# Latent attention: context products on unsplit F32 rows in column halves, with row sums added on DVE and POOL

## The reference

```python
B, S, L, H = 16, 100, 1444, 16           # batches, queries, keys, heads
D_CQ, D_C, R = 192, 64, 64
q_big = apply_rope(einsum('bshk,hkq->bshq', (x @ Wq.T), w_kc_q))
kv_r  = apply_rope(kv_c)                                   # (B, L, 64), shared by all heads
q_r = einsum('bshq,hqr->bhsr', q_big, W_qr)
k_r = einsum('bld,hdr->bhlr', kv_r, W_kr)
attn  = softmax(einsum('bhsr,bhlr->bhsl', q_r, k_r))
ctx_c = einsum('bhsl,bld->bhsd', attn, kv_r)               # per head 100 x 64
out   = (einsum('bhsd,hkd->bhsk', ctx_c, w_kc_kv)) @ Wo.T
```

## Time and profile before

| | us |
|---|---|
| median of 3 runs | 2277.09 (2274.82 to 2286.96) |
| the profiled execution | 2283.25, its span 2281.4 |
| latent queries | about 76 to 306 of the span |
| latent attention | about 308 to 1370, its first turn of maxima at 354.4 |
| PE busy over the span | 1857.9 (81%) |
| DVE, ACT, POOL busy | 1492.1, 1220.5, 1117.1 |
| mean granted TensorE clock | 0.905 of full speed |

### The profile page before, as it was taken

One profiled execution on the slowest core, in us unless ns is written; L12 is line 12 of the kernel. 1 busy time (PEld: TensorE's weight loads), 2 busy tenths in 40 slices (PEclk: granted clock), 3 DMA queues, 4 the chain that ended last, 5 costly groups with the idle time before them and its releaser, 6 DMA issues. The chain is left out here.

```text
span 2281.4 us, 38538 instructions
## 1 busy us (share of the span) xinstructions
PE 1857.9 (81%) x10550; PEld 1632.6 (72%) x10550; DVE 1492.1 (65%) x2799; ACT 1220.5 (53%) x2996; POOL 1117.1 (49%) x961
## 2 busy tenths in 40 slices
PE   4999958999999999999999973499993689837870
PEld 3677736888888888888888963499993466626870
DVE  4677777777777777767776433377774466656763
ACT  2111115777777767767777851366661266515650
POOL 0455528888788888878888852300004100014005
PEclk9999967999999999999999985699996599958985
DMA  5522251111111111111110002455542100026654
GB/s 159 197 58 57 55 176 55 63 63 63 45 54 63 64 31 63 63 64 63 63 54 11 16 8 78 140 197 196 204 165 58 34 1 0 0 77 196 198 164 113
DMA packets 115748, 195.76 MB, mean 86 GB/s; under 512 B 48213, under 2 KB 94265, under 8 KB 110161
## 3 DMA queue, kind: packets, MB, share of 16 engines
q1 hardware_dynamic: 107409, 180.88, 24.6%
q0 software_dynamic: 8192, 13.15, 2.0%
HBM read 147.01 MB, written 46.63 MB: 85 GB/s over the span
## 5 line engine op out<-in xcount | busy, mean ns | idle before, releaser
L501 POOL TENSOR_TENSOR EL<-E,EH 128x400 fp32r<-128x400 f32 x688 | 833.4, 1239 | 158.5 <-ACT EH L733 154.0
L599 DVE TENSOR_REDUCE PM<-bank 128x1 f32<-128x482 f32 (+1 forms) x624 | 397.2, 650 | 185.9 <-PE bank L578 182.9
L742 ACT ACTIVATE E<-bank 128x400 f32<-128x400 f32 x768 | 386.4, 503 | 212.8 <-PE bank L793 153.2
L733 ACT ACTIVATE EH<-E 128x400 fp32r<-128x400 f32 x768 | 407.0, 532 | 0.0
L175 PE MATMUL bank<-EH,KVH 128*128 128x400 f32 x768 | 283.1, 369 | 19.8 <-POOL EL L501 18.5
L578 PE MATMUL bank<-KH,QS 128*128 128x482 f32 (+1 forms) x624 | 250.9, 414 | 53.9 <-DVE KVL L549 27.6
L1248 POOL DMA_INDIRECT m_back<-rows_out,m_slots x64 | 64.8, 1013 | 450.8 <-DMA rows_out<-m_ys 421.2
L792 PE MATMUL bank<-QS,KH 128*128 128x400 f32 x768 | 272.1, 354 | 14.9 <-issue 9.1
L793 PE MATMUL bank<-QB,KB 66*128 66x400 f32 x768 | 269.1, 350 | 0.0
L175 PE MATMUL bank<-EH,KVL 128*128 128x400 f32 x768 | 265.7, 346 | 0.0
L175 PE MATMUL bank<-EL,KVH 128*128 128x400 f32 x768 | 265.5, 346 | 0.0
(11 more groups left out here) (244 smaller groups left out, 3983.3 us busy)
## 6 DMA issues: line engine op xcount, KB each, us to landing
m_stage_u<-in_m_up SPq DMA_DIRECT2D x20, 1392.0 KB
raw<-in_ctx_T SPq DMA_DIRECT2D x16, 1444.0 KB, 6.1
m_xg<-rows_in SPq DMA_DIRECT2D x55, 256.0 KB, 4.1
rows_out<-m_ys SPq DMA_DIRECT2D x55, 256.0 KB, 3.7
m_stage_d<-in_m_down SPq DMA_DIRECT2D x20, 696.0 KB
queries<-q_out SPq DMA_DIRECT2D x64, 200.0 KB, 2.4
QS<-queries SPq DMA_DIRECT2D x16, 800.0 KB, 6.1
rows_in<-zeros SPq DMA_DIRECT2D x5, 1792.0 KB
```

The lines of the kernel that those rows point to most:

```text
L501: ops.tensor_tensor(EL[:, n % PB, :], E[:, n % EB, :], as_f32(EH[:, n % PB, :]), ALU.subtract).then_inc(sem, 1)
L599: nc.vector.tensor_reduce(PM[:, f:f + 1], psum[F0 + f % f_banks(b)][:, 0:KW[f % KC]], AX.X, ALU.max).then_inc(red_done, 1)
L733: nc.scalar.activation(EH[:, n % PB, :], E[:, n % EB, :], ACT.Copy).then_inc(hi_done, 1)
L742: nc.scalar.activation(E[:, n % EB, :], psum[S0 + n % SB][:, 0:CH], ACT.Exp).then_inc(exp_done, 1)
```

## The change

- **Values** are plain F32: KV (rotated, unsplit) against the exponentials R, unsplit. A batch has two parts p of eight heads, NS = 24 steps of (p, key tile). Each step has two score tiles, one of the four even heads of the part and one of the odd ones, 400 columns each, read as strided heads from QS and QB. The value product of the even heads goes to partitions 0 to 63 of bank CTX, that of the odd heads to 64 to 127. Each has a 64-column stationary operand. High copies (L733), EL (L501) and the columns of ones go.
- **Row sums**: DVE adds the even heads' tiles one by one in a PSUM bank (ACC), POOL the odd heads' tiles in SBUF (EA). The last addition writes ES, and TensorE multiplies a matrix of ones (64 wide) with it, two F32 matmuls a part. ACT copies them to SU.
- **Padding keys** are switched off by a row of -1e30 in KB instead of the ones column.
- **Order**: TensorE works in groups of two steps: a pair of maximum pieces, four scores, a pair of maximum pieces, the values of the two steps before. Maximum pieces are all 482 wide (overlapping), and DVE reduces two in one instruction.
- **Rotation** of the keys moves from DVE to POOL, but for two parts; the division is one instruction of 128 partitions.
- **Latent queries**: two heads share a bank, the even head in partitions 0 to 63, the odd one in 64 to 127; ACT and DVE then work once for two heads, and four DMAs store them.
- QB and KB have 128 rows; the memsets before the loop are larger.

```diff
@@ latent_queries
-                    for half in range(2):
-                        last = nc.tensor.matmul(psum[4 + h % 2][:, 0:CH], M2[:, half, h, :], rot[:, h % TURNS, half, :],
-                                                start=half == 0, stop=half == 1)
+                    for half in range(2):
+                        for o in range(2):
+                            h = 2 * j + o
+                            last = nc.tensor.matmul(psum[4 + j % 2][o * DC:(o + 1) * DC, 0:CH], M2[:, half, h, :],
+                                                    rot[:, h % TURNS, half, :], start=half == 0, stop=half == 1)
@@ latent_attention
-    EB, PB = 4, 6
-    BEHIND = 4
+    EB = 8
+    S0, F0, CTX, ACC, MISC = 0, 3, 5, 6, 7
+    SUM_AT, SUM0_AT, OUT_AT, TURN_AT = 2, 8, 9, 10
+    RECIP_AT, CT_AT = 9, 14
+    ROT_AT = (3, 4, 5, 6, 8, 9, 10, 11, 13, 14)
+    HI_AT, LO_AT = (17, 18), (18, 20)
@@ max_pair, reduce_pair
+            for f in pieces(i):
+                t, j = divmod(f, KC)
+                last = nc.tensor.matmul(psum[f_bank(b, i) + f % 2][:, 0:KW], QS[r][:, t * P:(t + 1) * P],
+                                        KH[r][:, KAT[j]:KAT[j] + KW], start=True, stop=True)
+            last.then_inc(f_ready, 1)
+            nc.vector.tensor_reduce(PM[:, 2 * i:2 * i + n], banks[:, k:k + n, 0:KW], AX.X, ALU.max).then_inc(red_done, 1)
@@ sums
+        def sum_even(v, b, n):
+            p, t = divmod(n, KT)
+            v.wait_ge(exp_done, b_val(b) * 2 * NS + (2 * n + 1 + SB))
+            v.wait_ge(even_sum, b_val(b) * NS + (EB + n))
+            acc = psum[ACC][:, 0:CH]
+            if t == 0:
+                ins = nc.vector.tensor_copy(acc, tile_of(n, 0))
+            elif t < KT - 1:
+                ins = nc.vector.tensor_tensor(acc, acc, tile_of(n, 0), ALU.add)
+            else:
...
+                ins = nc.vector.tensor_tensor(ES[:, p, 0, :], acc, tile_of(n, 0), ALU.add)
+            ins.then_inc(even_sum, 1)
+        def sum_odd(pool, b, n):
...
+            nc.gpsimd.tensor_tensor(out, first, tile_of(n, 1), ALU.add).then_inc(odd_sum, 1)
+        def sums(pe, b, p):
...
+            for o in range(2):
+                last = nc.tensor.matmul(psum[MISC][o * DC:(o + 1) * DC, 0:CH], ones[:], ES[:, p, o, :], start=True, stop=True)
+            last.then_inc(sum_done, 1)
@@ scalar
-                        nc.scalar.activation(E[:, n % EB, :], psum[S0 + n % SB][:, 0:CH], ACT.Exp).then_inc(exp_done, 1)
-                        if n:
-                            high(b, n - 1)
+                        act.wait_ge(av_done, b_val(b) * NS + (n + 1))
+                        act.wait_ge(even_sum, b_val(b) * NS + (n + 1))
+                        for o in range(2):
+                            act.wait_ge(s_ready, b_val(b) * 2 * NS + (2 * n + o + 1))
...
+                            nc.scalar.activation(tile_of(n, o), psum[S0 + (2 * n + o) % SB][:, 0:CH], ACT.Exp).then_inc(exp_done, 1)
@@ tensor
+                def values(b, n):
+                    p, t = divmod(n, KT)
+                    pe.wait_ge(exp_done, b_val(b) * 2 * NS + (2 * n + 2 + SB))
+                    if t == 0:
+                        pe.wait_ge(cu_done, b_val(b) * 2 + (p + 1))
+                    for o in range(2):
+                        last = nc.tensor.matmul(psum[CTX][o * DC:(o + 1) * DC, 0:CH], KV[b_mod(b)][:, t, :], tile_of(n, o),
+                                                start=t == 0, stop=t == KT - 1)
+                    last.then_inc(av_done, 1)
+                def step(b, has_next, has_keys):
+                    for m in range(NS // 2):
+                        if has_next and m == 0:
+                            pe.wait_ge(k_ready, b_val(b) + 2)
...
+                        if has_next and 2 * m < NP:
+                            max_pair(pe, b + 1, 2 * m)
+                        if m == 0:
+                            if b is not FIRST:
+                                for n in range(NS - 2, NS):
+                                    values(before(b), n)
+                            pe.wait_ge(m_in, b_val(b) * 32 + 32)
+                        for n in (2 * m, 2 * m + 1):
+                            scores(b, n)
+                        if has_next and 2 * m + 1 < NP:
+                            max_pair(pe, b + 1, 2 * m + 1)
...
+                        for n in (2 * m - 2, 2 * m - 1):
+                            if n >= 0:
+                                values(b, n)
@@ vector, before the loop
+                    v.memset(as_f32(QB[r][0:DC, :]), 0.0)
+                    v.memset(as_f32(KB[r][0:DC, :]), 0.0).then_inc(rows_set, 1)
+                    v.memset(as_f32(QB[r][0:1, :]), 1.0)
+                    v.memset(as_f32(KB[r][0:3, :]), 1.0).then_inc(rows_set, 1)
+                    v.memset(as_f32(KB[r][0:1, 0:SK]), 0.0)
+                    v.memset(as_f32(KB[r][0:1, SK:]), PAD).then_inc(pads, 1)
```

More of the change, by code:

```diff
@@ L52, in __init__ @@
         self.nc, self.ctx = nc, ctx
-        self.psum = [ctx.enter_context(nc.psum_tensor(f"bank{i}", [P, PSUM_COLS], F32)) for i in range(8)]
+        self.banks = ctx.enter_context(nc.psum_tensor("banks", [P, 8, PSUM_COLS], F32))
+        self.psum = [self.banks[:, i, :] for i in range(8)]
         self.stats = fixed(ctx, nc, "stats", [S, B, 6])
@@ L551, in rotate_part, with keys_high @@
-            ins.then_inc(rot_step, 1)
-        def keys_high(act, b, part, step):
+                ins = ops.tensor_tensor(KB[r][DC:, half], raw[DC:, 0, half], as_f32(KH[r][DC:, half]), ALU.subtract)
+            ins.then_inc(k_ready if i == ROT else rot_step, 1)
+        def keys_high(act, b, part):
             half = slice(part * KR, (part + 1) * KR)
             act.wait_ge(rot_step, b_val(b) * ROT + 9)
-            if step is not None:
-                act.wait_ge(av_done, b_val(step) * NS + PB)
@@ new lines, in sums, with sums_out @@
+        def sums(pe, b, p):
+            pe.wait_ge(even_sum, b_val(b) * NS + (EB + KT * (p + 1)))
+            pe.wait_ge(odd_sum, b_val(b) * 2 * ADDS + ADDS * (p + 1))
+            if p == 0 and b is not FIRST:
+                pe.wait_ge(su_done, b_val(b) * 2)
+            for o in range(2):
+                last = nc.tensor.matmul(psum[MISC][o * DC:(o + 1) * DC, 0:CH], ones[:], ES[:, p, o, :], start=True, stop=True)
+            last.then_inc(sum_done, 1)
+        def sums_out(act, b, p):
+            act.wait_ge(sum_done, b_val(b) * 2 + (p + 1))
+            if b is not FIRST:
+                act.wait_ge(sr_in, b_val(b) * 32)
+            nc.scalar.activation(SU[:, p, :], psum[MISC][0:DC + 1, 0:CH], ACT.Copy).then_inc(su_done, 1)
@@ new lines, in step @@
+                        for o in range(2):
+                            act.wait_ge(s_ready, b_val(b) * 2 * NS + (2 * n + o + 1))
+                            if o and n >= EB:
+                                act.wait_ge(odd_sum, odd_sums_to(b, n - EB))
+                            elif o and b is not FIRST:
+                                act.wait_ge(odd_sum, odd_sums_to(before(b), NS + n - EB))
+                            nc.scalar.activation(tile_of(n, o), psum[S0 + (2 * n + o) % SB][:, 0:CH], ACT.Exp).then_inc(exp_done, 1)
@@ L771, in _, with scores @@
                 turn_max(pe, FIRST)
+                def scores(b, n):
+                    r = b_mod(b)
+                    p, t = divmod(n, KT)
+                    keys = slice(t * P, (t + 1) * P)
+                    for o in range(2):
+                        pe.wait_ge(exp_done, b_val(b) * 2 * NS + (2 * n + o + 1))
+                        out = psum[S0 + (2 * n + o) % SB][:, 0:CH].rearrange("p (j s) -> p j s", s=S)
+                        for lhs, rhs in ((KH, QS), (KB, QB)):
+                            heads = rhs[r][:, p * 2 * CH:(p + 1) * 2 * CH].rearrange("p (j o s) -> p o j s", o=2, s=S)
+                            last = nc.tensor.matmul(out, lhs[r][:, keys], heads[:, o], start=lhs is KH, stop=lhs is KB)
+                        last.then_inc(s_ready, 1)
@@ L808, in step @@
                             turn_max(pe, b + 1)
-                steps(pe, step)
-                for n in range(NS - BEHIND, NS):
-                    values(Batch(0, B - 1), n)
-                project(pe, Batch(0, B - 1))
+                        for n in (2 * m - 2, 2 * m - 1):
+                            if n >= 0:
+                                values(b, n)
+                        if m == SUM_AT and b is not FIRST:
+                            sums(pe, before(b), 1)
+                        if m == SUM0_AT:
+                            sums(pe, b, 0)
+                        if m == OUT_AT and b is not FIRST:
+                            pe.wait_ge(su_done, b_val(b) * 2 + 1)
+                            project(pe, before(b))
+                steps(pe, step)
+                for n in range(NS - 2, NS):
+                    values(LAST, n)
+                pe.wait_ge(res_done, B - 1)
+                sums(pe, LAST, 1)
+                pe.wait_ge(su_done, 2 * B)
```

(1 more changed line is left out.)

393 lines of the change are left out of this document (180 added, 213 removed).

## The result

The changed kernel takes 2204.81 us, median of four runs (2200.92 to 2232.34), against 2280.26 of the kernel before in its four (2274.82 to 2286.96): a ratio of 0.969, with a 95% interval of 0.961 to 0.978. It is faster by 75 us. The profiled execution took 2204.48 us with a span of 2202.7.

A forecast was written before the change was run, and what follows sets the result against it. TensorE sets the attention's period, 62.5 us a batch, POOL close behind. Terms of -81-7+7+1-25-2 = -107 us took the 2277 median to 2170, set at 2180 for unseen waits; 8-in-10 range 2105 to 2420.

The forecast's parts named there:

- Values: Attention: two steps' eight F32 value passes overlap into five slots of 0.34 us; 20.4 us a batch against 26.2 before.
- four slots: Within the rival of overlap with nearly free width changes (chance 0.16): one step's passes pair fully, another -70 us.
- Latent queries: Before the attention: two heads' products take five slots, 1.70 us instead of 2.72; -25 us, and -2 for the folding.
- Changes of width: Attention: TensorE goes from 128-wide to 64-wide work and back 24 times a batch, 0.12 us each, 2.9 us.
- The turn: Attention's 13-wide turn of the row maxima, once a batch; read as hardly 0.05 us for a width change.
- Sums: Attention: two pairs of F32 sum matmuls on TensorE, three slots each, 2.0 us a batch.
- Fourth score: Attention: the fourth score in a row waits for the first exponential, 0.15 us a group, 1.8 us a batch.
- It is covered: Attention: the divisors' chain SR, RR, RS, some 12 us from step 5 to 14, precedes the project at step 18.
- ACT holds exp, copies and keys: Attention rival, chance 0.09: the halves overlap, but a new wait of 5 us a batch takes the gain; 2265 us.
- The wait on DVE goes: Attention: TensorE's wait on DVE's maxima, 1.6 us a batch, goes, since a pair's banks are read before the next pair.
- Before the loop: Memsets of 23 us against 12.7 start the first products 10 us later; a 3.5 us stop goes; +7 in all.
- Busy shares: Attention: POOL at 0.7, DVE at 0.7 and ACT at 0.5 busy, none of them reaching TensorE.

## Why the prediction was right, and where it was off

The sign, the mechanism of the gain and the range hold: forecast -107 us against the profiled execution, measured -78.7 (some 7 of it outside the change). That the number is near is in part luck, as the sum below shows. The steps one by one:

- **Values: right mechanism, the term too large.** Five slots, 20.4 us a batch, were taken between 16.1 and 32.6; it is four slots, 16.1. The fifth slot came from the assumed order of issue, and no row showed it. What was named only within a rival ("four slots") is what the trace shows. By the prediction's own price for it, -70 us, the forecast would have been 2110 and not 2180, and further off. Shown twice: by the loss when both halves write the same partitions, and by the order that makes no difference.
- **Latent queries: -25 and -2 forecast, -27 measured** when they stand alone. Two heads take 6.04, not 6.34, by the same fourth slot, less dearer changes.
- **Changes of width: too small.** 0.12 taken, 0.17 read off the starts, 4.1 us a batch instead of 2.9, near the folding's price. The split groups give 0.13 to 0.20. The turn was the wrong neighbour; why its 13-wide product costs less is not shown.
- **Sums 2.0, measured 1.35:** two slots in place of three, by the same overlap. **Fourth score 0.15, measured 0.13 a group; maxima 8.5, scores 17.5: as forecast.** The projection was read as 3.3 and costs 3.45, before the change as after it.
- **"It is covered": the step that failed.** The prediction followed the divisors from sums to RS and found them done before the project at step 18. They were. It did not follow the buffer that the division empties: the next contexts are copied into it at ACT's step 13, the division is at DVE's step 14. It did name the case among the rivals ("ACT holds exp, copies and keys"), but looked for the late part in POOL's sums, and gave it 0.09. The place is right, the reason another: no sum was late, and with POOL's additions cut nothing changes. Its price, 2.5 us of wait and in most batches 1.65 of slow clock, took nearly all that values and sums gave beyond the forecast. The run with the division moved shows 3.4 a batch.
- **"The wait on DVE goes": half right.** 25.5 us became 19.2, one stop of 1.25 in each of the 15 periods, for the first group has no values between its second pair and the next one. The forecast's "1.5 us of scores later" holds for the other groups and not for that one.
- **Before the loop: +10 forecast, +18.4 measured** from the end of the latent queries to the first turn: memsets +14.6, 2.8 until they begin, 1.8 for the first maxima, a little less for the rotation. The "first score near 370" was given on the clock of before; less the 27 us of the latent queries that is 343, and it is 351. The time lost comes back partly: the first period is 49.8 us where 61.1 had been.
- **Busy shares:** POOL 0.63 and DVE 0.65 of the stage's window for 0.7, ACT 0.42 for 0.5. None of the three is the bound, as was said.

An ordinary batch adds up to 17.5 + 16.1 + 8.5 + 1.35 + 3.45 + 0.1 + 4.1 + 1.6 = 52.7, and with 4.2 for the stop on ACT and 1.25 on DVE 58.1 of the 58.6. The other 0.5 is not assigned. In the forecast the same batch, without loop edges, had 56.5. It came out near since an over-sized term (4.3 us) and two missed stops (5.4) were of one size, and that is luck.

## What to carry to other kernels

When two 64-wide F32 products share a moving size, give them different output halves before anything else: with the sums in SBUF on both sides it decided here between ratios of 1.00 and 1.08. When an order is rewritten, follow each buffer to who fills it next, not only each value to who reads it; the costly wait was the write into CU, not the read of the divisors. And where two engines add at the same time, look at where each operand lies before counting both at their price alone.

## What the hardware showed that was not expected

- Two 64-wide F32 passes of different output halves start 6 to 13 ns apart, also when the kernel issues four passes of the one half ahead of the first of the other.
- A change between 64-wide and wider work cost TensorE 0.17 us, also where both sides are plain F32. A change between plain F32 and fp32r at full width cost nothing that the starts show.
- DVE's F32 addition of 128 x 400, both operands in SBUF, beside POOL doing the same: 824 ns in the median, up to 2068, against 574 with POOL's additions cut and 573 with one operand in PSUM. POOL's own goes from 1040 to 1138. The whole program lost some 80 us by it.
- Of the 14 stops of TensorE of 2.5 us in a busy stretch, 11 were followed by a stretch at 1.2 GHz (granted clock 0.50; 3.3 us behind the one at 916.9). No stop of 1.25 us was, in this kernel; with both halves in the same partitions some were, as the one that ends at 501.2 us (0.50 from 501.9). In the run with the values after each step, whose stops in this stretch are 1.25 us and shorter, the clock was 1.00 from 420 to 1240 us.
- The stop of 3 to 4 us that the profile puts down to "issue" at loop edges is absent when the values follow every step, and under 1 us when both halves write the same partitions.
